# A GRU, an expert mixture and a sampling grid on one core: one bias row split last, the last block's x and weights in another order, its tail summed by part of the width

## The reference

```python
hs = GRU(x, h0=cond_2048, W_ih, W_hh, b_ih, b_hh)          # 512 steps, one after the other
# layer 0: a base matrix, and for each row the best 2 of 8 low-rank experts (rank 16)
x1 = x + hs @ weight.T + sum_e w_e * (hs @ lora_A[e].T) @ lora_B[e].T * 2
# the second condition: x1 sampled along the width at positions given by cond_2048
s = w0 * x1[..., i0] + w1 * x1[..., i0 + 1]
# layer 1: for each row of s the best 2 of 8 experts, 512 -> 2 * 512 -> 512
h = s @ w1[e].T + b1[e]; y = h_glu * sigmoid(1.702 * h_glu) * (h_lin + 1)
out = x1 + sum_e r_e * (y @ w2[e].T + b2[e])
```

## Time and profile before

| | |
|---|---|
| median of 3 runs | 1869.8 us (1867.73 to 1875.03) |
| the profiled execution, its own time | 1869.3 us |
| its span | 1867.5 us |
| TensorE busy | 1694.5 us, 91% |
| VectorE busy | 1298.7 us, 70% |
| ScalarE busy | 780.2 us, 42% |
| DMA, mean over the span | 179 GB/s |
| first recurrence step's products | 28.60 us |
| last recurrence step's end | about 1670 us |
| last sum | 1863.12 us |

### The profile page before, as it was taken

One profiled execution on the slowest core, in us unless ns is written; L12 is line 12 of the kernel. 1 busy time (PEld: TensorE's weight loads), 2 busy tenths in 40 slices (PEclk: granted clock), 3 DMA queues, 4 the chain that ended last, 5 costly groups with the idle time before them and its releaser, 6 DMA issues.

```text
span 1867.5 us, 95461 instructions
## 1 busy us (share of the span) xinstructions
PE 1694.5 (91%) x40986; PEld 1153.0 (62%) x40986; DVE 1298.7 (70%) x5788; ACT 780.2 (42%) x2714; POOL 299.0 (16%) x600
## 2 busy tenths in 40 slices
PE   6888888878889999989799999989799999988998
PEld 5777677666556666656566666656566666664444
DVE  6888788887767776767776767777777677764323
ACT  5655566643333444333334444432334444323442
POOL 2222222221211111021211110121311111022001
PEclk8999999999999999999999999999999999999999
DMA  7436445444436667625336667426346666449994
GB/s 258 144 132 218 155 158 189 171 157 149 133 99 186 199 211 211 184 77 149 122 107 195 198 211 215 142 87 167 110 123 200 197 201 189 136 104 387 388 355 144
DMA packets 176689, 334.06 MB, mean 179 GB/s; under 512 B 46448, under 2 KB 46600, under 8 KB 176264
## 3 DMA queue, kind: packets, MB, share of 16 engines
q1 hardware_dynamic: 171144, 311.17, 52.0%
q0 software_dynamic: 5120, 16.78, 2.8%
HBM read 263.10 MB, written 64.78 MB: 176 GB/s over the span
## 4 chain that ended last, share of the span: by engine, by line
PE 67%; DVE 16%; ACT 6%; issue 5%; DMA 3%; SPq 2%; DVEq 0%; POOL 0%; ACTq 0%
PE bank_g L682 16%; PE bank L968 14%; PE bank_g L687 12%; PE bank_g L698 7%; PE bank L988 7%; DVE xt L1440 5%; DVE na L1446 3%; DVE pre L1442 3%; ACT rz L1114 3%; DVE hs_early L1452 3%; ACT seq_h L1114 3%; PE bank L724 2%; DMA wih<-x_rows 2%; PE bank L950 1%; PE bank L964 1%
## 5 line engine op out<-in xcount | busy, mean ns | idle before, releaser
L1842 POOL COPY hxs<-hs 128x32 f16<-128x32 f16 x512 | 224.7, 439 | 1325.9 <-DVE hs L1460 1325.9
L1114 ACT ACTIVATE rz<-pre 128x32 f32<-128x32 f32 x512 | 125.9, 246 | 732.2 <-DVE pre L1442 731.4
L682 PE MATMUL bank_g<-whh,hs_early 128*32 128x256 f16 x8192 | 318.5, 276 | 123.9 <-DVE hs_early L1452 120.4
L1440 DVE STREAM_TRANSPOSE xt<-bank_g 128x256 f32<-128x256 f32 x512 | 231.0, 451 | 208.9 <-PE bank_g L687 198.9
L682 PEld LDWEIGHTS bank_g<-whh,hs_early 128*32 128x32 f16 x8192 | 171.5, 96 | 313.9 <-DVE hs_early L1452 304.7
L698 PE MATMUL bank_g<-whh,hs 128*32 128x128 f16 x16384 | 325.4, 219 | 10.3 <-issue 9.3
L687 PE MATMUL bank_g<-whh,hs 128*32 128x256 f16 x8192 | 313.5, 273 | 0.1
L968 PE MATMUL bank<-wm,wih 128*128 128x512 f16 x1272 | 309.6, 381 | 2.9 <-issue 2.3
L698 PEld LDWEIGHTS bank_g<-whh,hs 128*32 128x32 f16 x16384 | 257.7, 97 | 16.8 <-issue 15.5
L687 PEld LDWEIGHTS bank_g<-whh,hs 128*32 128x32 f16 x8192 | 203.7, 96 | 22.5 <-DVE hs L1460 3.2
L1114 ACT ACTIVATE seq_h<-na 128x16 f32<-128x16 f32 x512 | 114.8, 224 | 207.5 <-DVE na L1446 206.8
(11 more groups left out here) (245 smaller groups left out, 2026.3 us busy)
## 6 DMA issues: line engine op xcount, KB each, us to landing
wm<-moe_split SPq DMA_DIRECT2D x318, 512.0 KB, 4.6
wm<-in_w_moe SPq DMA_DIRECT2D x32, 768.0 KB, 5.7
moe_split<-wm SPq DMA_DIRECT2D x32, 768.0 KB, 5.1
wih<-x_rows SPq DMA_DIRECT2D x58, 256.0 KB, 4.8
y_rows<-wih SPq DMA_DIRECT2D x58, 256.0 KB, 4.7
whh<-moe_split SPq DMA_DIRECT2D x24, 512.0 KB
gi<-moe_split SPq DMA_DIRECT2D x18, 512.0 KB, 6.8
xr<-in_x SPq DMA_DIRECT2D x16, 512.0 KB, 4.6
```

The costliest lines, as they stand in the source:

```text
L682: mm(out_strip(0, j, 2 * P), early_cols[:, 8 * B * k:8 * B * (k + 1)], strip(whh[:, 1, k, 0:2 * D], j), start=(k == 0), stop=False)
L1114: return nc.scalar.activation(dst, src, func, **kw)
L1440: link(V.transpose(rows, bank_g[0][:, 0:2 * P].rearrange("p (m c) -> p m c", c=32)))
L1842: Q.tensor_copy(hxs[:, par, :, :, :, col].rearrange("p s k b -> p s (k b)"), hs_new).then_inc(S["h_kept"], 1)
```

## The change

Four edits.

1. *Bias row.* One copy of b_hh's n part is loaded in place of two, behind W_hh in SyncE's queue. ScalarE casts it after all the input gates, VectorE makes the low half in row 32 from row 0, after W_hh's third part. The clearing of `bias_f` by GpSimd goes.
2. *x1 over x.* In the last block the sums go to `xr`, over x (`sums`), and the last gathers go to `x1`, so `x1_sum` doesn't wait for the store of block 2 there; the last gathers do.
3. *Weights of the last block.* SyncE waits for the gathers of block 2, loads tiles 0 and 1, then waits for the recurrence's end, loads x, then tiles 2 and 3, each followed by half of block 2's store. The rows of tiles 2 and 3 are loaded by ScalarE, in tile 0, behind a wait for all scatters.
4. *Held sums by part.* The four banks stand for the parts k of the width, with all four batch rows in 512 columns; they are begun by the bias product (scaled by AS through `mixt`), so `turn_back` in the last block is transposes alone. The banks no longer collide with those of `turn_back`. The order on TensorE, ScalarE and VectorE is another, `held_zero` isn't used, and `store_last` stores part by part, each part when all batch rows are in.

```diff
-bias_f = x1_f[0:2 * 32, 3 * D:4 * D]
+bias_f = x1_f[0:1, 3 * D:4 * D]
...
-got = [[xr_f[:, b * D:(b + 1) * D], x1s_f32[:, b * D:(b + 1) * D]] for b in range(B)]
+sums = [x1] * (FB - 1) + [xr]
+got = [[[v[:, b * D:(b + 1) * D], x1s_f32[:, b * D:(b + 1) * D]] for b in range(B)]
+       for v in [xr_f] * (FB - 1) + [x1_f]]
...
-turned = [bank_g[0], bank_g[1], bank_l[1], bank[3]]
+turned = [bank_g[0], bank_g[1], bank_l[0], bank[2]]
...
-added = [bank[0], bank[1], bank_g[0], bank_g[1]]
+added = [bank[0], bank[1], bank[3], bank_l[1]]
...
-    sp.wait_ge(S["bias_zero"], 1)
-    for row in range(2):
-        sp.dma_start(bias_f[32 * row:32 * row + 1, :].rearrange("o (m p) -> o m p", m=K),
-                     b_hh[:, 2 * K:].rearrange("p (o m) -> o m p", o=1),
-                     allow_slow_non_contiguous=True).then_inc(S["bias_row_in"], 16)
     for q in range(3):
         sp.dma_start(part_of(wm32[1], q), part_of(w_hh, q)).then_inc(whh_in[q], 16)
+    sp.dma_start(bias_f.rearrange("o (m p) -> o m p", m=K), b_hh[:, 2 * K:].rearrange("p (o m) -> o m p", o=1),
+                 allow_slow_non_contiguous=True).then_inc(S["bias_row_in"], 16)
...
     def store_last(f):
-        for b in range(B):
-            sp.wait_ge(S["final_done"], f * B + b + 1)
+        for k in range(K):
+            sp.wait_ge(S["half_done"], (6, 6, 7, 8)[k])
             for q in range(2):
-                sp.dma_start(out[2 * f + q, :, :, b * TB:(b + 1) * TB], x1[:, :, b, q * TB:(q + 1) * TB]
-                             ).then_inc(S["out_stored"], 16)
+                sp.dma_start(out[2 * f + q, :, k].rearrange("p (b t) -> p b t", b=B),
+                             sums[f][:, k, :, q * TB:(q + 1) * TB]).then_inc(S["out_stored"], 16)
...
     f = FB - 1
-    sp.wait_ge(S["h_ready"], FB * FT + 1)
-    for q in range(2):
-        load_block(f, q)
-    for q in range(2):
-        store_out(f - 1, q)
-    for j in range(LAST_RING):
+    for b in range(B):
+        sp.wait_ge(gathered[b], f * 32)
+    for j in range(2):
         for n in range(K):
             load_up(f, j, n)
         for n in range(2):
             load_down(f, j, n)
+    sp.wait_ge(S["h_ready"], FB * FT + 1)
+    for q in range(2):
+        load_block(f, q)
+    for j in range(2, LAST_RING):
+        for n in range(K):
+            load_up(f, j, n)
+        for n in range(2):
+            load_down(f, j, n)
+        store_out(f - 1, j - 2)
     sp.wait_ge(S["scattered"], FB * B * 2 * 16)
-    load_rows(f, 2)
-    load_rows(f, 3)
...
-    def add_held(f, i, b):
-
-        if i == 0:
-            if b > 1:
-                pe.wait_ge(S["half_done"], b - 1)
-            mm(added[b][:, :], held_zero, held_t[0][:, 0].rearrange("p b n -> p (b n)"), start=True, stop=False,
-               skip_group_check=True)
+    def add_bias(f, k):
+
+        mm(added[k][:, :], b2w[:, k * P:(k + 1) * P], mixt[:, :, :].rearrange("e b n -> e (b n)"),
+           start=True, stop=False, skip_group_check=True)
+
+    def add_held(f, i, k):
+
         pe.wait_ge(S["held_lo"], i + 1)
-        for k in range(K):
-            for w, a in PARTS:
-                r = mm(added[b][:, k * P:(k + 1) * P], held_y[i][:, a, k], held_t[i][:, w, b], start=False,
-                       stop=(i == HELD - 1 and a == 1), skip_group_check=True)
+        for w, a in PARTS:
+            r = mm(added[k][:, :], held_y[i][:, a, k], held_t[i][:, w].rearrange("p b n -> p (b n)"),
+                   start=False, stop=(i == HELD - 1 and a == 1), skip_group_check=True)
         if i == HELD - 1:
...
         for k in range(K):
-            nc.tensor.transpose(banks[b][:, k * P:(k + 1) * P], got[b][0][:, k * P:(k + 1) * P], idt[:, :])
-            r = mm(banks[b][:, k * P:(k + 1) * P], b2w[:, k * P:(k + 1) * P], mixt[:, b],
-                   start=False, stop=True, skip_group_check=True)
+            r = nc.tensor.transpose(banks[b][:, k * P:(k + 1) * P], got[f][b][0][:, k * P:(k + 1) * P], idt[:, :])
+            if f < FB - 1:
+                r = mm(banks[b][:, k * P:(k + 1) * P], b2w[:, k * P:(k + 1) * P], mixt[:, b],
+                       start=False, stop=True, skip_group_check=True)
...
     def last_end(f):
 
         pe.wait_ge(S["held_out"], HELD)
+        pe.wait_ge(S["y_done"], (f + 1) * NT)
+        pe.wait_ge(S["mix_out"], f + 1)
+        for k in range(K):
+            add_bias(f, k)
         add_held(f, 0, 0)
-        add_held(f, 0, 1)
         down(f, NT // 2, 0, 3)
         down(f, NT // 2, 0, 4)
-        for b in range(2):
-            turn_back(f, b, turned)
-            if b:
-                add_held(f, 1, b - 1)
-            add_held(f, 0, b + 2)
+        turn_back(f, 0, turned)
+        turn_back(f, 1, turned)
+        for k in range(1, K):
+            add_held(f, 0, k)
         turn_back(f, 2, turned)
-        add_held(f, 1, 1)
+        for k in range(2):
+            add_held(f, 1, k)
         turn_back(f, 3, turned)
-        add_held(f, 1, 2)
-        add_held(f, 1, 3)
+        for k in range(2, K):
+            add_held(f, 1, k)
...
         scaled(1)
+        scaled(2)
         y_held(f, 1)
-        scaled(2)
         scaled(3)
...
+            if f == FB - 1 and j == 0:
+                act.wait_ge(S["scattered"], FB * B * 2 * 16)
+                for n in (2, 3):
+                    act.dma_start(xg[n % 2], x_rows[n * P:(n + 1) * P]).then_inc(rows_in[n % 2], 16)
...
-    act.wait_ge(S["bias_row_in"], 16 * 2)
-    act.wait_ge(S["bias_zero"], 2)
-    run(bias_n[0:2 * 32], bias_f, ACT.Copy, scale=WS).then_inc(S["bias_hi"], 1)
     whh_hi(1)
     for m in range(6, 9):
         gi_out(0, m)
     whh_hi(2)
     for m in range(9, G3):
         gi_out(0, m)
+    act.wait_ge(S["bias_row_in"], 16)
+    act.wait_ge(S["bias_zero"], 1)
+    run(bias_n[0:1], bias_f, ACT.Copy, scale=WS).then_inc(S["bias_hi"], 1)
...
             dve.wait_ge(S["block_in"], (f + 1) * 32)
-            if f:
+            if 0 < f < FB - 1:
                 dve.wait_ge(S["out_stored"], f * 32)
         dve.wait_ge(S["l0_mm"], f * K + o + 1)
-        stt_(x1[:, o].rearrange("p b t -> p (b t)"), bank[o][:, :], 1 / PS,
+        stt_(sums[f][:, o].rearrange("p b t -> p (b t)"), bank[o][:, :], 1 / PS,
              xr[:, o].rearrange("p b t -> p (b t)"), ALU.mult, ALU.add).then_inc(S["x1_done"], 1)
...
-            stt_(got[b][0], got[b][1], kept_p[:, b, 1:2], got[b][0], ALU.mult, ALU.add
+            stt_(got[f][b][0], got[f][b][1], kept_p[:, b, 1:2], got[f][b][0], ALU.mult, ALU.add
...
-        def add_back(b):
+        def add_back(b, n):
             dve.wait_ge(S["back_mm"], f * B + b + 1)
-            tt_(x1[:, :, b], turned[b][:, :].rearrange("p (k t) -> p k t", k=K), x1[:, :, b], ALU.add
+            if n:
+                dve.wait_ge(S["half_done"], n)
+            tt_(sums[f][:, :, b], turned[b][:, :].rearrange("p (k t) -> p k t", k=K), sums[f][:, :, b], ALU.add
                 ).then_inc(S["half_done"], 1)
 
-        def add_held(b):
-            dve.wait_ge(S["held_mm"], HELD + b + 1)
-            dve.wait_ge(S["half_done"], b + 1)
-            stt_(x1[:, :, b], added[b][:, :].rearrange("p (k t) -> p k t", k=K), 1 / AS, x1[:, :, b],
-                 ALU.mult, ALU.add).then_inc(S["final_done"], 1)
+        def add_held(k, n):
+            dve.wait_ge(S["held_mm"], HELD + k + 1)
+            dve.wait_ge(S["half_done"], n)
+            x_k = sums[f][:, k].rearrange("p b t -> p (b t)")
+            stt_(x_k, added[k][:, :], 1 / AS, x_k, ALU.mult, ALU.add).then_inc(S["half_done"], 1)
 
         combine(0)
         combine(1)
+        combine(2)
+        add_back(0, 0)
         y_held(1)
-        add_back(0)
-        combine(2)
-        add_back(1)
-        add_held(0)
+        add_back(1, 1)
+        add_back(2, 2)
         combine(3)
-        add_back(2)
-        add_held(1)
-        add_back(3)
-        add_held(2)
-        add_held(3)
+        add_held(0, 3)
+        add_held(1, 4)
+        add_back(3, 5)
+        add_held(2, 6)
+        add_held(3, 7)
...
-    dve.wait_ge(S["bias_hi"], 1)
-    low = slice(32, 32 + 1)
-    stt_(bias_n[low], bias_f[low], WS, bias_n[low], ALU.mult, ALU.subtract).then_inc(S["bias_row"], 1)
     whh_lo(1)
     whh_lo(2)
+    dve.wait_ge(S["bias_hi"], 1)
+    stt_(bias_n[32:32 + 1], bias_f, WS, bias_n[0:1], ALU.mult, ALU.subtract).then_inc(S["bias_row"], 1)
...
             pool.wait_ge(S["sample_mm"], (f + 1) * B)
             if f == FB - 1:
                 pool.wait_ge(S["held_prob"], 1)
-        Q.indirect_dma_start(got[b][c], None, y_rows,
+                pool.wait_ge(S["out_stored"], f * 32)
+        Q.indirect_dma_start(got[f][b][c], None, y_rows,
...
-    Q.memset(bias_f, 0.0).then_inc(S["bias_zero"], 1)
```

16 lines of the change are left out of this document (8 added, 8 removed).

## The result

The changed kernel takes 1876.15 us (median of 22 runs, 1872.60 to 1880.61) against 1873.23 us for the kernel before (22 runs, 1867.73 to 1876.47). The ratio, taken over all these runs, is 1.0021 with a 95% interval of 1.0014 to 1.0028, which is 3.9 us more; the two medians alone are 2.9 us apart. The forecast was +1.2 us on a median of 1869.8 us, with a range of 1862 to 1876 us. With more runs that median itself came out at 1873.2; on the forecast's scale the ratio gives 1873.7 us. So the class (no change by 0.5%) and the sign are as forecast, the size isn't, and the median lies just beyond the range. The profiled execution took 1874.75 us, its span is 1873.0 us (before 1867.5). One execution of a later run, e12, took 2325.3 us at a mean granted clock of 0.69, and its ratio leaves that one out.

What follows compares the result with a forecast made beforehand. TensorE was busy 91% of the span, its 512 recurrence steps untouched, so only start, hand-over and tail could move: -2.1 + 4.7 - 1.1 = +1.5 us on 1869.3, 1870.8 us (1871 on the median's scale), range 1862 to 1876.

Steps and rivals of the forecast that it cites:

- Class and sign: Whole kernel: no change beyond 0.5%, chance 0.92, and by the sum slightly slower, +1.5 us.
- part 2: Hand-over: x1 over x and early weights; +6.8 us at the first sum, -2.1 at tile 2's rows, together +4.7 us.
- so it lands at about 1688.5 ... +6.8 us: Hand-over: x lands behind twelve weight pieces (6.29 MB), delaying the first x1 sum by 6.8 us (bounds +5, +8.5).
- Follow rigidly: Hand-over: sums, resampling, routing and tile 0's pick shift with the first sum; first up product from 1703.3 to 1710.1.
- Rows of tiles 2 and 3: Hand-over: issued by ScalarE, they land 3 to 4 us later, before they are wanted; TensorE's 2.11 us wait goes, -2.1 us.
- rival (b): Hand-over: rows of tiles 2 and 3 come late, deciding from a 6.0 us landing on; 1874.5 us; chance 0.15.
- Late waits: Last block from tile 8: SyncE's rounds outlast TensorE's tiles, so x_rows stays 2.2 us late; term 0 (to -2.2).
- Rival (c): Last block: waits of 0.32, 0.61 and 1.29 us come from DMA backlog, not SyncE's pace; 1868.8 us; chance 0.15.
- Rival (a): Hand-over: x does not queue behind the weights, first sum at 1678.4, -2.9 instead of +6.8; 1861 us; chance 0.15.
- Part 1: Start: one bias row behind W_hh, split last, brings step 0's pre sooner; -2.1 us (bounds -3.9, -0.5).
- both cost nothing as long as x is the last to come: Start: ScalarE's bias cast (0.6 us) and VectorE's low half (0.7 us) fit beside the wait for x, at no cost.
- Part 3: Tail: held sums by part, last sum 2.7 us sooner, but stores need all four blocks; -1.1 us (bounds -2.5, 0).

Runs made afterwards that it cites:

- e12: e11 and e10 together; ratio 0.9939 (0.9922-0.9955) to the kernel before.
- set 2: Second of four sets of runs, on one chip with the kernel before timed beside it; holds e5, e6 and e7; ratios 0.9931 to 0.9992.
- e1: Changed kernel with the last block's two x loads ahead of all weight pieces; ratio 0.9984 to the kernel before.
- e2: Changed kernel with only tile 0's six weight pieces ahead of x, tile 1's behind it; ratio 0.9984 to the kernel before.
- e9: Changed kernel unaltered, timed again in another set on a third chip; ratio 1.0021 to the kernel before.
- e10: Changed kernel with GpSimd loading the bias row in four pieces, its split ahead of W_hh's last third, 10 idle products; ratio 1.0019 to the kernel before.
- e6: Changed kernel with tile 0's four up pieces ahead of x, no h_ready wait before x, rows as in e5; ratio 0.9931 to the kernel before.
- e5: Changed kernel with rows of tiles 4 to 14 issued by ScalarE too, one tile earlier in the code; ratio 0.9977 to the kernel before.
- e7: Changed kernel with 13 idle products on TensorE in step 0, ahead of the bias row wait; ratio 0.9992 to the kernel before.
- e15: e11 with x ahead of all weights; ratio 0.9942 (0.9925-0.9959) to the kernel before.
- e11: e6 with block 2's two stores moved from behind tiles 2 and 3 to the turns of tiles 1 and 2; ratio 0.9926 to the kernel before.
- e13: Changed kernel with the last block's x loads issued by ScalarE, twelve weight pieces ahead on SyncE as changed; ratio 1.0061 to the kernel before.
- e14: e11 with all twelve weight pieces begun at once and x loaded by ScalarE; ratio 1.0049 to the kernel before.

## Why the prediction was right and where it was wrong

- **Class and sign, right, the sign in part by luck.** No change by 0.5%, and slightly slower: part 2 costs more than parts 1 and 3 bring. In set 2, where part 2 costs 1.9 us, no run shows the changed kernel slower. What the forecast didn't have is that this cost depends on a stand of TensorE that set 2's traces lack.
- **The failed step: "so it lands at about 1688.5 ... +6.8 us".** The mechanism (x behind 6.29 MB in SyncE's queue) was right, by e1, e2 and the table; the size wasn't. The first sum came 21.6 us after the last step (20.9 and 21.3 in e9 and e10) where I had 18.5 (18.7 by my own sum), so the term is +9.7, outside its bounds (+5, +8.5). The 2.9 us that were missing have three parts. The pieces ended 15.0 us after the last step, not 13.6: 1.4 us. From there x took 6.6 us, not 5.5, with the 2 us at 105 GB/s in the middle: 1.1 us. And the 0.4 us that I took off for overlap weren't there. The second load of x was held at issue; I had that as the upper bound and priced it too low, because rows 5 show x's issue with nothing ahead of it (2.04 us). "Follow rigidly" was nearly right: by the first up product it was +10.8 (the resampling ran at half clock after 12.76 us of standing, 6.84 us for 18 products, 5.74 before), of which the up products at full clock gave 1.7 back (2.76 us for 12; before, 4.45).
- **Rows of tiles 2 and 3, right in result, wrong in size.** The wait of 2.11 us is gone. But they landed 7.0 and 8.7 us after issue, not 3 to 4. My own bound for rival (b) was 6.0 us; they were just in time only because TensorE reached tile 2 some 7.1 us after the issue, later than forecast, which is luck. In e6, where x is early, the wait is back with 2.69 us, and ScalarE stands 3.26 us at the scatters: rival (b)'s mechanism.
- **Late waits, right.** 0.17 + 2.24 us against 2.22, and they go when ScalarE issues the rows (e5): it was SyncE's late issue. Rival (c) falls.
- **Rival (a) falls**: x does queue.
- **Part 1: -2.1 forecast, -3.1 at step 0, -1.6 at step 5.** The step "both cost nothing as long as x is the last to come" failed: TensorE stood 3.25 us for the split on VectorE, its clock fell, and step 1's `hs_early` came 4.70 us after step 0's instead of 3.36. In e7, where the clock stayed up, late expert weights and a stand of TensorE took the same again. The traces with part 1 have -1.5 to -2.7 at step 5, so the forecast lies within their scatter. Not seen either: wherever in SyncE's queue the row stands, the load behind its small packets is held (the second row 6.93 us in the kernel before, b1 8.57 us in the changed one).
- **Part 3: -1.1, right.** It is -0.7 from the last down product on and -0.4 ahead of it: 5.33 us from the down product before, where the kernel before has 5.74, from the row below to 1850.39. The last sum comes 1.9 us sooner, not 2.7, but the stores end the kernel, as forecast: they can't begin before `add_back(3)`.

```profile
1844.65 2.75 PE L988 MATMUL bank<-wm,wih 128*128 128x512 f16 x12
```

- **Sum.** With +9.7 and -1.6 in place of +6.8 and -2.1 the sum is +4.9 us; the two clock items (+1.1 and -1.7) make it +4.3, against +3.9 measured.

## What to carry to other kernels

A load that is begun early in an in-order queue is paid for by what stands behind it: put the load that ends the next wait first, and look whether anything else waits behind bulk (here `x_rows`; taking it off that queue, with the stores later, made x's earlier landing count, 0.9942 in e15 against 0.9984 in e1 on the same chip). Loads of many small packets should neither stand behind bulk in their own queue nor go beside it on another. And when a stage's first wait goes, ask which load is the next to be late before the gain is booked.

## What the runs showed that I had not expected

- A load can be held at its issuer for long: 8.57 us behind the load of 512 single floats (itself 2.59 us to issue), and for the two loads of x 4.3 to 6.5 us behind four pieces of weights (e6, e11, e12), 7.06 behind six (e2), 10.66 behind twelve, against 1.8 to 2.1 us with nothing ahead. On ScalarE's own queue, with nothing ahead there but SyncE's bulk on the engines, they took 7.16 and 7.93 us (e13, e14).
- 1.05 MB in 256-byte packets on a second queue took up to 28.4 us beside bulk, 6.2 us alone.
- In set 2's traces the recurrence took 1617.3 to 1618.6 us, in the others 1620.3 to 1627.6, and part 2 cost a third there. Set 2 had a chip to itself, but one set doesn't show that the chip is the cause; nor is it shown what TensorE stands for where the traces say `<-issue`.
- e6 and e11 beat both kernels: 0.9931 (0.9919 to 0.9944) and 0.9926 (0.9911 to 0.9941). So do e12 and e15, with 0.9939 and 0.9942.
